# Pair products split into a rounded half and a remainder, with layer 0 in three fp32r products

## The chip, the cores and the metric

The kernel runs on 1 core of one Trainium2 chip. The metric is the device time in microseconds, the median of several executions; lower is better. The profiler followed one further execution of the kernel before.

## The reference

A batch of 1024 rows has 39 fields, each an embedding of 16 numbers that is looked up in its own table. A compressed interaction network of three layers combines them, and a small network follows.

```
x0 = e                       # (1024, 39, 16), gathered from 39 tables
for W in (f0, f1, f2):       # f0 (39*39, 128), f1 and f2 (128*39, 128)
    z  = einsum('bfd,bgd->bfgd', x0, xk).reshape(b, f*g, d)
    xk = einsum('bpd,pm->bmd', z, W)
    outs.append(xk)
z = sum(concatenate(outs, 1), -1)          # (1024, 384)
h = relu(concatenate([z, dense_ctx], 1) @ W_top1 + b_top1)
h = relu(h @ W_top2 + b_top2)
y = h @ W_top3
```

## The kernel before, in words

The batch is cut into 8 batch tiles of 128 rows (index bt), each batch tile into 4 groups of 32 rows (index q; g = 4*bt + q counts the 32 groups), and each group into 4 tiles of 8 rows (index j; t counts the 128 tiles). Eight rows times 16 embedding numbers fill the 128 partitions of a tile. Every engine runs a list of instructions written out by hand, and semaphores tie the lists together.

**Layer 0** uses the symmetry of x times x. The 39*40/2 products of two fields are laid out in 7 blocks (k = 0 to 6) of up to 117 partitions: `pairs[k] = x shifted by k fields * base`, 512 columns wide (32 rows times 16). SyncE copies `base` and the six `shifted` blocks of each group by DMA. GpSimd multiplies them (`pair`, L347); for the first group VectorE does it (L536). TensorE sums the seven blocks into bank C, one fp32 matmul each, with the folded filter `f0_sum` (`cur0_sum`, L655); the trace has two records for each such matmul. The matmuls for group g + 1 are put into group g's list at the slots AT_SUM = 12, 15, ..., 30 of 40 slots. `pairs` is a ring of 3, and a product waits for the sum that frees its place.

**The split of cur0.** ScalarE rounds the sum to fp32r (`cur0_high`, L423), and VectorE takes the remainder (`cur0_low`, L540) and the sum over the 16 embedding numbers for the output (`z0`, L542). ScalarE does it in tile 3 at c = 1, VectorE there ahead of the reduction of unit 2.

**Layer 1** is the bulk. Per tile there are 10 chunks (c = 0 to 9) of 4 fields, a slot each: TensorE multiplies cur0 with f1 in three fp32r matmuls of 512 columns (L707, L708, L709) into one of 6 PSUM banks. Two chunks form a unit. The chunks of units 0, 2 and 4 are scaled by x on ScalarE (L436), and VectorE reduces the unit (L577, L585, L596). The other chunks are scaled and added by VectorE itself (`fuse`, L572, alternating between `sum_a` and `sum_b`). L587 adds the reduced unit 2 to `sum_a`, and L593 adds `sum_a` and `sum_b` into the last unit. TensorE may write a unit again once VectorE has read what stood there three units earlier; chunk 4 of a tile waits for L596 of the tile before.

**Layer 2 and the rest.** For each tile, `g_product` (L663) multiplies the result with `x_block`, which GpSimd spreads from `x_col` (L331, four instructions for a group); ScalarE copies it to G (L428, at c = 5). Layer 2 (L669) sums over 39 fields, 13 in each of the groups q = 1, 2, 3 of the next batch tile, in bank C; the small network uses bank C in the groups with q = 0, and once more in the last group. The first instruction of a group waits for `cur0_low`, and a use of bank C also for `z0`.

**Loading.** GpSimd gathers the rows of the next batch tiles (L320, 39 indirect DMAs for a batch tile), spread over the tiles. SyncE repeats the gathered rows by DMA (L291), and TensorE transposes them in the group with q = 2 (L629; L714 for the first batch tile, copied from PSUM at L399 and L522). At the start SyncE issues 50 loads of f0 and ScalarE 47 more of its mirror (L227), and the weights f2, w1 and w2 follow on SyncE ahead of the first copies of x.

Of the kernel before, what the change touches and what calls it, by code (L numbers as in the profile page):

```python
# [5 lines left out]
F32 = mybir.dt.float32  # L6
F32R = mybir.dt.float32r
# [26 lines left out]
RING = 3  # L34
# [19 lines left out]
AT_SUM = [12 + 3 * k for k in range(K0)]  # L54
# [6 lines left out]
EARLY = 16  # L61
AHEAD = 10
# [52 lines left out]
def gathers_in_tile(t):  # L115


    step, u = divmod(t + AHEAD, TPB)
    if step == 0:
        n, tiles = NF - EARLY, TPB - AHEAD  # L120
        return 1, range(EARLY + n * t // tiles, EARLY + n * (t + 1) // tiles)
    if step + 1 >= BT:
        return None
    return step + 1, range(NF * u // TPB, NF * (u + 1) // TPB)


def build(nc, dense, ids, tables, w1, b1, w2, b2, w3, f0, f1, f2, out):
    ctx = ExitStack()
    with ctx:
# [12 lines left out]
        f0_sum = sb("f0_sum", [SEL, K0, M])  # L142
# [11 lines left out]
        rows = sb("rows", [P, 2, SEQ * D])  # L154
# [4 lines left out]
        pairs = sb("pairs", [SEL, RING, GN])  # L159
        cur0_high = sb("cur0_high", [P, 2, GN], F32R)  # L160
# [5 lines left out]
        part = sb("part", [P, 2, M])  # L166
# [6 lines left out]
        dense_sb = G[:, FC * P + K0 * M:FC * P + K0 * M + BT * D].rearrange("p (t c) -> p t c", t=BT)  # L173
# [5 lines left out]
        y = sb("y", [1, B])  # L179
# [6 lines left out]
        gathered = [sem("gathered_even"), sem("gathered_odd")]  # L186
        consts_made, block_ready, ones_set = sem("consts_made"), sem("block_ready"), sem("ones_set")
        mirror_zero, f0_in, f0_ready = sem("mirror_zero"), sem("f0_in"), sem("f0_ready")
        f1_in, f1_high_ready, f1_ready = [sem(f"f1_in{i}") for i in range(3)], sem("f1_high_ready"), sem("f1_ready")
# [3 lines left out]
        first_repeat, repeated, x_read = sem("first_repeat"), sem("repeated"), sem("x_read")  # L193
        based = [sem("based_even"), sem("based_odd")]
        copied = [sem(f"copied{k}") for k in range(1, K0)]
        first_pairs, pairs_ready = sem("first_pairs"), sem("pairs_ready")
        cur0_summed, cur0_high_ready, cur0_ready = sem("cur0_summed"), sem("cur0_high_ready"), sem("cur0_ready")
# [25 lines left out]
        def load_f0(eng, mirrored):  # L223
            for mirror, k, p0, n, first, step in pieces:
                if mirror == mirrored:
                    dst = (f0_mirror if mirror else f0_sum)[p0:p0 + n, k, :]
# [15 lines left out]

        def base_copy(eng, g, j):
# [3 lines left out]

        def shift_copy(eng, g, k):
            cols = x_cols(*divmod(g, QG))
            r = K0_ROWS[k]  # L250
            eng.dma_start(shifted[0:r, k - 1, :], cols[k:k + r, :]).then_inc(copied[k - 1], 16)
# [4 lines left out]
        def _(sp):  # L256
            sp.dma_start(ids_sb[:], ids.rearrange("(t p) f -> p t f", p=P)).then_inc(ids_in, 16)
            load_f0(sp, False)
            sp.dma_start(f2_sb[:], f2.rearrange("(f g) m -> g f m", g=M)).then_inc(f2_in, 16)
# [562 lines left out]
```

## Time and profile before

| | |
|---|---|
| median of 3 runs | 1467.61 us (1467.0 to 1467.76) |
| the profiled execution, its own time | 1464.04 us |
| its span | 1462.3 us |
| mean granted TensorE clock | 0.971 |
| busy: PE, DVE, ACT, POOL | 92%, 83%, 62%, 46% |

PE is TensorE, PEld its weight loads, DVE VectorE, ACT ScalarE, POOL GpSimd and SP SyncE. Times are in microseconds from the start of the span. L587 is line 587 of the kernel before. Matmuls are pipelined and their ends are modelled, so distances between starts say more than durations.

### The profile page before, as it was taken

What the parts mean: (1) busy time and instruction counts of PE and PEld (TensorE: products, weight loads), DVE (VectorE), ACT (ScalarE), POOL (GpSimd) and SP (SyncE); (2) the same over time, 40 slices, a digit from 0 to 9 for tenths busy, and PEclk for the clock granted to TensorE, in tenths of its full rate; (3) what the DMA queues carried; (4) which work ended last, traced back from release to release, by engine and by line L of the source; (5) the groups of instructions that cost most, each with busy time, mean ns of one, the idle gap of its engine ahead of it and who ended that gap; (6) DMA issues with size and microseconds to landing.
All of it is one profiled execution on the core that took longest, in us unless ns stands there. A gap on an engine that the chain in (4) does not pass through costs nothing.

```text
span 1462.3 us, 20057 instructions
## 1 busy us (share of the span) xinstructions
PE 1344.7 (92%) x5856; PEld 1001.8 (69%) x5856; DVE 1212.5 (83%) x2792; ACT 907.2 (62%) x3233; POOL 676.1 (46%) x666
## 2 busy tenths in 40 slices
PE   0059999999999999999999999999999998988998
PEld 0036676667777777777777777777777676766677
DVE  0249999998989999899889989898989989898874
ACT  0226776666666676667666676666766665655563
POOL 6737656554445555554545547354545423123200
PEclk8579999999999999999999999999999999999999
DMA  7131212120300212010210202101210202010000
GB/s 181 35 109 29 66 45 69 27 65 3 92 27 21 66 50 63 27 52 16 80 33 27 65 21 85 34 26 42 73 40 27 64 1 94 21 38 24 1 1 1
DMA packets 54456, 67.28 MB, mean 46 GB/s; under 512 B 13927, under 2 KB 25945, under 8 KB 54346
## 3 DMA queue, kind: packets, MB, share of 16 engines
q1 hardware_dynamic: 36811, 59.70, 12.9%
q0 software_dynamic: 9984, 2.58, 1.6%
q10 hardware_dynamic: 7551, 3.72, 1.0%
q8 instruction: 47, 0.77, 0.2%
q14 instruction: 63, 0.52, 0.1%
HBM read 10.02 MB, written 0.00 MB: 7 GB/s over the span
## 4 chain that ended last, share of the span: by engine, by line
PE 69%; DVE 17%; issue 5%; ACT 5%; ACTq 2%; another core or an unknown queue 1%; DMA 0%; SPq 0%; DVEq 0%
PE Y L707 16%; PE Y L709 14%; PE Y L708 14%; PE C L655 9%; PE C L669 5%; PE S L663 5%; DVE sum_b L572 4%; ACT Y L436 4%; DVE cur L596 4%; DVE sum_a L572 3%; DVE Y L593 2%; DVE part L585 2%; ACTq L227 2%; PE S L629 1%
## 5 line engine op out<-in xcount | busy, mean ns | idle before, releaser
L436 ACT ACTIVATE Y<-Y,x_col 128x128 f32<-128x128 f32 x2944 | 800.8, 356 | 447.2 <-PE Y L709 415.9
L707 PE MATMUL Y<-f_high,cur_high 128*128 128x512 f32 (+1 forms) x1280 | 627.6, 490 | 32.2 <-DVE cur L596 23.2
L709 PE MATMUL Y<-f_high,cur_low 128*128 128x512 f32 (+1 forms) x1280 | 500.1, 391 | 0.0
L708 PE MATMUL Y<-f_low,cur_high 128*128 128x512 f32 (+1 forms) x1280 | 499.6, 390 | 0.0
L347 POOL TENSOR_TENSOR pairs<-shifted,base 117x512 f32<-117x512 f32 x186 | 241.0, 1296 | 548.5 <-PE C L655 546.6
L572 DVE SCALAR_TENSOR_TENSOR sum_a<-Y,x_col,sum_a 128x128 f32<-128x128 f32 x1024 | 349.6, 341 | 13.9 <-issue 0.5
L707 PEld LDWEIGHTS Y<-f_high,cur_high 128*128 128x128 f32 x1280 | 242.4, 189 | 171.0 <-DVE cur L596 57.9
L320 POOL DMA_INDIRECT rows<-in_tbl_dram,ids_sb x312 | 304.1, 975 | 72.4 <-issue 58.9
L572 DVE SCALAR_TENSOR_TENSOR sum_b<-Y,x_col,sum_b 128x128 f32<-128x128 f32 x896 | 305.1, 341 | 0.5 <-DVE sum_a L572 0.4
L708 PEld LDWEIGHTS Y<-f_low,cur_high 128*128 128x128 f32 x1280 | 243.1, 190 | 84.9 <-issue 47.4
L709 PEld LDWEIGHTS Y<-f_high,cur_low 128*128 128x128 f32 x1280 | 241.5, 189 | 51.7
L655 PE MATMUL C<-pairs,f_sum 117*128 117x512 f32 (+1 forms) x448 | 230.0, 596 | 6.7 <-DVE pairs L536 6.7
L585 DVE TENSOR_REDUCE part<-Y 128x128 f32<-128x1024 f32 x128 | 156.5, 1223 | 74.3 <-ACT Y L436 72.1
L577 DVE TENSOR_REDUCE sum_a<-Y 128x128 f32<-128x1024 f32 x128 | 155.9, 1218 | 35.2 <-ACT Y L436 34.7
L596 DVE TENSOR_REDUCE cur<-Y 128x128 f32<-128x1024 f32 x128 | 156.7, 1224 | 4.4
L655 PEld LDWEIGHTS C<-pairs,f_sum 117*128 117x128 f32 (+1 forms) x448 | 84.7, 192 | 29.7 <-issue 10.2
L331 POOL TENSOR_TENSOR x_block<-x_col,block 128x320 f32<-128x320 f32 x128 | 91.3, 745 | 9.0 <-ACT x_col L417 8.5
L587 DVE TENSOR_TENSOR sum_a<-sum_a,part 128x128 f32<-128x128 f32 x128 | 88.7, 693 | 4.4
L663 PE MATMUL S<-x_block,cur 128*128 128x320 f32 x256 | 92.2, 442 | 0.0
L669 PEld LDWEIGHTS C<-G,f_sb 128*128 128x128 f32 x624 | 84.0, 196 | 10.1 <-issue 3.6
L669 PE MATMUL C<-G,f_sb 128*128 128x128 f32 x624 | 86.1, 280 | 1.4 <-ACT G L428 0.6
L593 DVE TENSOR_TENSOR Y<-sum_a,sum_b 128x128 f32<-128x128 f32 x128 | 66.9, 523 | 14.0 <-ACT Y L436 0.8
(73 smaller groups left out, 554.6 us busy)
## 6 DMA issues: line engine op xcount, KB each, us to landing
shifted<-x_seq SPq DMA_DIRECT2D x157, 234.0 KB
base<-x_seq SPq DMA_DIRECT2D x96, 78.0 KB
rows<-in_tbl_dram,ids_sb POOLq DMA_INDIRECT x312
shifted<-x_seq SPq DMA_DIRECT2D x32, 156.0 KB
rows<-rows SPq DMA_DIRECT2D x14, 312.0 KB
G<-in_L_rec_f_dram ACTq DMA_DIRECT2D x3, 832.0 KB
w_sb<-in_W_top_dram SPq DMA_DIRECT2D x1, 768.0 KB
shifted<-x_seq ACTq DMA_DIRECT2D x3, 234.0 KB
```

Of the source, the lines that this page charges most:

```text
L320: pool.indirect_dma_start(out=rows[:, bt % 2, f * D:(f + 1) * D], out_offset=None, in_=tables[f], in_offset=bass.IndirectOffsetOnAxis(ap=i ...
L347: pool.tensor_tensor(pairs[0:r, z % RING, :], shift, base[0:r, g % 2, :], ALU.mult)\
L436: ins = act.activation(where[:, i * M:(i + 1) * M], where[:, i * M:(i + 1) * M], ACT.Copy, scale=x_col[:, t // JT % QG, t % JT, f:f + 1])
L572: dve.scalar_tensor_tensor(acc, src, x, acc, ALU.mult, ALU.add).then_inc(acc_steps, 1)
L585: dve.tensor_reduce(part[:, t % 2, :], unit(t, 2), AX.X, ALU.add).then_inc(acc_steps, 1)
L596: dve.tensor_reduce(cur1[:, t % 2, :], unit(t, 4), AX.X, ALU.add).then_inc(acc_steps, 1)
L655: pe.matmul(C[:], f0_sum[0:r, k, :], pairs[0:r, z % RING, :], start=k == 0, stop=k == K0 - 1).then_inc(cur0_summed, 1)
L663: pe.matmul(S[:, 0:TB * FC], cur1[:, t % 2, :], x_block[:, t // JT % 2, t % JT, :], start=True, stop=True).then_inc(s_filled, 1)
L669: ins = pe.matmul(C[:, 0:P], f2_sb[:, f, :], half[:, f, :], start=f == first, stop=f == end - 1)
L707: pe.matmul(where, ch, wh, start=True, stop=False)
L708: pe.matmul(where, ch, wl, start=False, stop=False)
L709: pe.matmul(where, cl, wh, start=False, stop=True).then_inc(y_filled, 1)
```

## The change

Each pair product is now kept in three forms: the product in fp32 (`pairs`), its rounded half in fp32r (`pairs_high`, made by ScalarE) and the remainder (`pairs_low`, subtracted by GpSimd, for the first group by VectorE). The folded filter is split in the same way (`f0_sum` and `f0_low`). A layer-0 sum is three fp32r matmuls instead of one fp32 matmul. All three rings have 2 places. The sums stand at slots 12, 15, 19, 23, 27, 31, 35, ScalarE rounds at AT_ROUND, and cur0's split moves from c = 1 to c = 5 of tile 3 on ScalarE and behind `fuse(t, 6)` on VectorE.

```diff
-RING = 3
+RING = 2
-AT_SUM = [12 + 3 * k for k in range(K0)]
+AT_SUM = [12, 15, 19, 23, 27, 31, 35]
+AT_ROUND = {(0, 1): 0, (0, 5): 1, (1, 1): 2, (1, 5): 3, (2, 1): 4, (2, 5): 5, (3, 1): 6}
+            def pair_low(g, k):
+                z = K0 * g + k
+                r = K0_ROWS[k]
+                pool.wait_ge(pairs_rounded, z + 1)
+                pool.tensor_tensor(pairs_low[0:r, z % RING, :], pairs[0:r, z % RING, :],
+                                   pairs_high[0:r, z % RING, :].bitcast(F32), ALU.subtract).then_inc(low_ready, 1)
+            LOW_STEPS = ((("pair", 0), ("pair", 1), ("low", 0), ("pair", 2), ("low", 1)),
+                         (("pair", 3), ("low", 2), ("pair", 4), ("low", 3)),
+                         (("pair", 5), ("low", 4), ("pair", 6), ("low", 5)),
+                         (("low", 6),))
...
+            def round_pair(g, k):
+                z = K0 * g + k
+                r = K0_ROWS[k]
+                if g:
+                    act.wait_ge(pairs_ready, z - K0 + 1)
+                else:
+                    act.wait_ge(first_pairs, k + 1)
+                if z >= RING:
+                    act.wait_ge(cur0_summed, z - RING + 1)
+                act.activation(pairs_high[0:r, z % RING, :], pairs[0:r, z % RING, :], ACT.Copy)\
+                   .then_inc(pairs_rounded, 1)
...
                         if c == 1:
                             if q == 2 and bt + 1 < BT:
                                 read_transposes(bt + 1, j)
-                            if j == JT - 1 and g + 1 < NG:
-                                split_cur0(g + 1)
                             if with_mlp:
                                 relu1(mlp, mlp + 1)
                         if c == AT_G:
+                            if j == JT - 1 and g + 1 < NG:
+                                split_cur0(g + 1)
                             if t:
                                 read_g(t - 1)
                             if with_mlp:
                                 relu2(mlp, mlp + 1)
+                        if (j, c) in AT_ROUND and g + 1 < NG:
+                            round_pair(g + 1, AT_ROUND[j, c])
...
                 fuse(t, 3, FUSE3, 0)
                 if j == 0 and q and g >= QG:
                     layer2_read(g // QG - 1, q - 1)
-                if j == JT - 1 and g + 1 < NG:
-                    split_cur0(g + 1)
                 dve.wait_ge(scaled, NSC * t + 4)
-                dve.tensor_reduce(part[:, t % 2, :], unit(t, 2), AX.X, ALU.add).then_inc(acc_steps, 1)
+                dve.tensor_reduce(part[:], unit(t, 2), AX.X, ALU.add).then_inc(acc_steps, 1)
                 dve.wait_ge(acc_steps, n0 + R1)
-                dve.tensor_tensor(sum_a[:, t % 2, :], sum_a[:, t % 2, :], part[:, t % 2, :], ALU.add)\
+                dve.tensor_tensor(sum_a[:, t % 2, :], sum_a[:, t % 2, :], part[:], ALU.add)\
                    .then_inc(acc_steps, 1)
                 fuse(t, 6, FUSE6, 1)
+                if j == JT - 1 and g + 1 < NG:
+                    split_cur0(g + 1)
                 fuse(t, 7, FUSE7, 1)
...
-                pe.matmul(C[:], f0_sum[0:r, k, :], pairs[0:r, z % RING, :],
-                          start=k == 0, stop=k == K0 - 1).then_inc(cur0_summed, 1)
+                high, low = pairs_high[0:r, z % RING, :], pairs_low[0:r, z % RING, :]
+                pe.matmul(C[:], f0_sum[0:r, k, :], high, start=k == 0, stop=False)
+                pe.matmul(C[:], f0_low[0:r, k, :], high, start=False, stop=False)
+                pe.matmul(C[:], f0_sum[0:r, k, :], low, start=False, stop=k == K0 - 1).then_inc(cur0_summed, 1)
```

These parts of the change stand in words:

- GpSimd goes through LOW_STEPS with a gather between two steps. A pair product waits for the remainder that used its place before, a rounding for the sum that did. Gathers of a batch tile keep out of tiles 2 and 3 of the group with q = 1.
- The gathered rows are kept once (`rows`). Four GpSimd copies (`take_rows`, in those tiles 2 and 3) put them into `rows_seq` in the order of the embedding numbers; SyncE's three repeating DMAs for a batch tile are gone. For the first batch tile ScalarE, VectorE (two) and GpSimd make the four copies.
- At the start, GpSimd issues 4 gathers of batch tile 1 behind its copy, waits for the first copies of x, issues two shift copies itself, and only then the 12 gathers that remain. ScalarE takes one base copy and two shift copies, SyncE two and two.
- ScalarE rounds f1 first and issues the 47 loads of f0's mirror behind that. VectorE adds f0 and copies the first rows ahead of f1's remainder. For the first group VectorE takes turns: pair product k, then remainder k - 1.
- The loads of f2, w1 and w2 move on SyncE from ahead of the first copies to behind group 1's shift copies.
- `y` holds one batch tile, and ScalarE sends it out for each, where SyncE sent it twice at the end.

## Rows read from the trace of the kernel before

**Rows 1.** The page: busy time and share of each engine, and the chain by engine.
```profile
PE 1344.7 (92%) x5856; PEld 1001.8 (69%) x5856; DVE 1212.5 (83%) x2792; ACT 907.2 (62%) x3233; POOL 676.1 (46%) x666
...
PE 69%; DVE 17%; issue 5%; ACT 5%; ACTq 2%; another core or an unknown queue 1%; DMA 0%; SPq 0%; DVEq 0%
```

**Rows 2.** Windows, one batch tile each: length, then PE, PEld, DVE, ACT, POOL busy.
```profile
918.20:1085.10 166.90, 165.54 (x733) 123.76 (x732) 148.31 (x348) 112.46 (x403) 85.43 (x83) 1.00 0.15 45
1085.10:1260.00 174.90, 167.67 (x734) 124.76 (x732) 156.16 (x349) 112.45 (x403) 59.80 (x57) 0.99 0.14 42
```

**Rows 3.** Timeline, tile 1 of group 15: start, us, engine, line, operation.
```profile
724.62 1.12 ACT L436 ACTIVATE Y<-Y,x_col 128x128 f32<-128x128 f32 x4 [1.43 <-PE Y L709]
...
727.73 0.46 ACT L428 ACTIVATE G<-S 128x320 f32<-128x320 f32 x1
...
727.87 1.23 DVE L585 TENSOR_REDUCE part<-Y 128x128 f32<-128x1024 f32 x1 [0.90 <-ACT Y L436]
...
727.92 1.02 PE L655 MATMUL C<-pairs,f_sum 117*128 117x512 f32 x2
...
729.01 0.40 PE L708 MATMUL Y<-f_low,cur_high 128*128 128x512 f32 x1
...
729.24 0.40 PE L709 MATMUL Y<-f_high,cur_low 128*128 128x512 f32 x1
```

**Rows 4.** Waits between 120 and 1390 us: total, times, longest.
```profile
ACT Y L436 <- PE Y L709: 391.9, 333, 6.6
...
PEld Y L707 <- DVE cur L596: 55.4, 56, 4.7
```

**Rows 5.** By line, L587 and L540: duration in ns, min/median/max.
```profile
L587 DVE TENSOR_TENSOR sum_a<-sum_a,part x128: 291/293/2095, 106.2 to 1438.5; 128x128 f32<-128x128 f32 x128
...
L540 DVE TENSOR_TENSOR cur_low<-C,cur_high x32: 678/680/692, 96.6 to 1394.6; 128x512 fp32r<-128x512 f32 x32
```

**Rows 6.** Timeline, groups 15 and 27: DVE's additions and POOL's products.
```profile
729.03 1.30 POOL L347 TENSOR_TENSOR pairs<-shifted,base 117x512 f32<-117x512 f32 x1 [0.53 <-PE C L655]
...
729.13 1.34 DVE L587 TENSOR_TENSOR sum_a<-sum_a,part 128x128 f32<-128x128 f32 x1
...
1235.92 4.55 DVE L593 TENSOR_TENSOR Y<-sum_a,sum_b 128x128 f32<-128x128 f32 x1
...
1236.33 2.76 POOL L331 TENSOR_TENSOR x_block<-x_col,block 128x320 f32<-128x320 f32 x4
...
1239.06 1.25 POOL L347 TENSOR_TENSOR pairs<-x_seq,base 117x512 f32<-117x512 f32 x1
```

**Rows 7.** Groups by form from 584.4 to 751.2 us: busy, mean ns.
```profile
L587 DVE TENSOR_TENSOR sum_a<-sum_a,part 128x128 f32<-128x128 f32 x16 | 12.0, 748 | 0.5
...
L593 DVE TENSOR_TENSOR Y<-sum_a,sum_b 128x128 f32<-128x128 f32 x16 | 5.8, 362 | 1.7
```

**Rows 8.** Timeline, DVE in tile 3 of group 14.
```profile
707.39 0.68 DVE L540 TENSOR_TENSOR cur_low<-C,cur_high 128x512 fp32r<-128x512 f32 x1
707.99 0.68 DVE L542 TENSOR_REDUCE z<-C 128x32 f32<-128x512 f32 x1
```

**Rows 9.** Timeline, the start up to the first chunk.
```profile
1.33 21.03 SPq L227 DMA_DIRECT2D f_sum<-in_L_rec_f_dram  x50
...
9.64 40.73 ACTq L227 DMA_DIRECT2D G<-in_L_rec_f_dram  x47
...
57.11 0.70 ACT L396 ACTIVATE rows<-rows 128x624 f32<-128x624 f32 x1
...
60.46 3.65 PE L714 MATMUL Y<-ident,rows 128*123 128x128 f32 x16 [37.42 <-DVE rows L518]
...
75.29 0.95 POOL L320 DMA_INDIRECT rows<-in_tbl_dram,ids_sb  x1 [0.31 <-issue]
...
79.81 0.29 DVE L522 COPY x_seq<-Y 123x128 f32<-123x128 f32 x1 [16.96 <-remote]
...
97.48 0.54 PE L707 MATMUL Y<-f_high,cur_high 128*128 128x512 f32 x1 [1.70 <-DVE cur_low L540]
```

More of the change, by code:

```diff
@@ L61 @@
 EARLY = 16
+FIRST_EARLY = 4
 AHEAD = 10
@@ L344, in pair @@
                 else:
-                    pool.wait_ge(copied[k - 1], 16 * (g + 1))
+                    pool.wait_ge(copied[k - 1], 16 * (g if k in POOL_COPIES else g + 1))
                     shift = shifted[0:r, k - 1, :]
+                if g == 1 and k < RING:
+                    pool.wait_ge(first_low, K0)
+                else:
+                    pool.wait_ge(low_ready, z - K0 - RING + 1)
                 pool.tensor_tensor(pairs[0:r, z % RING, :], shift, base[0:r, g % 2, :], ALU.mult)\
                     .then_inc(pairs_ready, 1)
+            def pair_low(g, k):
[8 more added lines that the diff above has]
+                         (("low", 6),))
             pool.wait_ge(ids_in, 16)
             gather(0, range(NF))
-            gather(1, range(EARLY))
+            pool.wait_ge(gathered, 16 * NF)
+            pool.tensor_copy(*row_part(2 * NF, NF)).then_inc(first_rows, 1)
+            pool.wait_ge(first_rows, 4)
+            gather(1, range(FIRST_EARLY))
+            pool.wait_ge(first_read, 4)
+            for k in POOL_COPIES:
+                shift_copy(pool, 0, k)
+            gather(1, range(FIRST_EARLY, EARLY))
             pool.wait_ge(ones_set, 1)
@@ L361, in _ @@
                     fs = list(now[1]) if now else []
-                    if now and now[0] == 2 and now[1][0] == 0:
-                        pool.wait_ge(first_filled, 4)
-                    elif now and now[0] > 2 and now[1][0] == 0:
-                        pool.wait_ge(s_filled, S_USE["x", now[0] - 2, JT - 1] + 1)
-                    ks = ((0, 1, 2), (3, 4), (5, 6), ())[j] if g + 1 < NG else ()
-                    for i in range(max(len(ks), len(fs))):
-                        if i < len(ks):
-                            pair(g + 1, ks[i])
+                    if now and now[0] > 1 and now[1][0] == 0:
+                        pool.wait_ge(rows_taken, len(ROW_PARTS) * (now[0] - 1))
+                    if q == 1 and j >= 2 and bt + 1 < BT:
+                        for part in ((0, 1), (2, 3))[j - 2]:
+                            take_rows(bt + 1, part)
+                    steps = LOW_STEPS[j] if g + 1 < NG else ()
+                    for i in range(max(len(steps), len(fs))):
+                        if i < len(steps):
+                            kind, k = steps[i]
+                            (pair if kind == "pair" else pair_low)(g + 1, k)
                         if i < len(fs):
@@ L402, in _ @@
             act.wait_ge(first_read, 4)
-            for k in (1, 3, 5):
+            base_copy(act, 0, 2)
+            for k in (1, 3):
                 shift_copy(act, 0, k)
```

177 lines of the change are left out of this document (110 added, 67 removed).

## The prediction

> **What bounds the kernel now.** I read the shares and the chain first. PE is busy for 92% of the span and holds 69% of the chain, DVE 83% and 17% [rows 1]. Then the stretches by batch tile of 16 tiles: the four from 417.5 to 1085.1 us take 166.8 to 167.0 us each, with PE at 165.4 to 165.5 and DVE at 148.0 to 149.2; the last of them is shown [rows 2]. PE's ends are modelled, so I counted its work by the distance from start to start. An fp32r product of 512 columns follows the last after 0.23 us, three make a chunk of 0.70 us, and an fp32 pair sum stands 0.86 us ahead of the next chunk's first product (from 727.92 us to 729.01 less the 0.23 that lie between 729.01 and 729.24) [rows 3]. A batch tile has 160 chunks (16 x 6.9 = 110), 16 G products of 0.53 (8.5), 28 pair sums (24), 39 layer-2 products of about 0.23 (9), the transposes of x and of the scalars (5.5) and the small network (6): about 162.5. So PE is idle for only 4.4 us of 167, and it spends them behind DVE: the longest of PE's waits, 55.4 us in 56 waits of its weight loads, is for the final reduce of L596 [rows 4]. The second engine is close behind the first, and what either waits for counts.
>
> The last view is how long DVE's two additions take whose operands all lie in SBUF. L587 has a minimum of 291 and a maximum of 2095 ns, while L540, which reads PSUM and SBUF, stays at 678 to 692 [rows 5]. The timeline shows why: L587 starts 0.10 us after a pair product of POOL and ends just behind it, 1.34 us long, and an L593 lasts 4.55 us through the rest of one pair product, four x_block products and the next pair product, which follow without a gap [rows 6]. In an undisturbed batch tile L587 and L593 have means of 748 and 362 ns [rows 7] against some 293 and 300 when nothing blocks them, so DVE loses 16 x (0.455 + 0.062) = 8.3 us. The price is in rows 2: from 918.2 to 1085.1 DVE is busy for 148.3 of 166.9 us, from 1085.1 to 1260.0 for 156.2 of 174.9. That is 7.9 us more for DVE and 8.0 more for the kernel: a blocked microsecond is paid about one to one.
>
> **Part 1, the pair sums on PE.** Three fp32r products at 0.23 replace one fp32 product: 0.86 - 0.70 = 0.16 us, 28 times in a batch tile: -4.4 us. The bounds are 0 (if the third weight load showed) and 0.16, which is what the chunks next to it show, so I take 0.16. The Trainium skill (FP8 and Floating Point Precision, on fp32 precision) says that true FP32 takes four passes through the array. By that rule a sum would fall from 0.86 to 0.64 and save 6 us in a batch tile; the chunks here show 0.70 for three.
>
> **Part 2, the later split of cur0.** Sum 6 moves from slot 30 to slot 35 of 40, and cur0's split from before the reduce L585 to behind fuse(6). Before, the split was over when PE came to the boundary: cur_low at 707.39, z at 707.99 [rows 8], a good microsecond ahead of the next group's first product. Now the chain starts at the end of chunk 35: ACT scales it (1.2, from the four in 1.12 us of rows 3), DVE reduces unit 2 (1.24), adds (0.3), fuses four (4 x 0.26), takes cur_low (0.68) and z (0.68): 4.5 us to cur_low, 5.2 to z. PE has 3 x 0.70 + 0.58 + 0.3 = 3.0 us of its own there. It idles 1.5 us where only cur_low is needed, and 2.2 where layer 2 or the small network needs bank C, which z must have read; from the second batch tile on that is every group. Against it I set 0.5 us of the idle that PE has now in such a tile and that falls away once DVE catches up at the boundary: +1.7 us for each of four groups, +6.8. Parts 1 and 2 make +2.4 for a batch tile. What is queued behind PE's wait is all of the next group.
>
> **Part 3, the remainder on POOL.** 28 subtractions of 117x512 in a batch tile. POOL's product of that shape takes 1.30 us [rows 6]; a subtraction isn't in the trace, and DVE's addition in L587 (128x128) against such a product can't tell more, so 1.30 with bounds 1.2 and 1.5. POOL goes from 85.4 us of 166.9 [rows 2] to about 122, and 127 with the copies of rows: not the bound. But where they lie matters. In tiles 0 to 2, ACT rounds a pair right behind G in slot c = 5, and POOL's subtraction starts as that ends. From G's start: G 0.46, the rounding 0.68 (as cur_low, which has its width [rows 8]; it is on ACT, so some hundredths may go either way), and POOL follows after 0.1: subtraction at +1.2. DVE's reduce L585 starts 0.14 after G, at 727.87 against 727.73, and L587 comes at 729.13, that is +1.4 us [rows 3, 6]. So L587 finds POOL at work for another 1.1 us, three times in four tiles and locked in phase, since both chains start from the same scaled chunk: 12 x 1.05 = 12.6 us. In tile 3 x_block's four products (2.8 us) and pair 0 now come when DVE wants L587, and a hit there delays cur_low: I put 4 us for a batch tile, and 1 for L593. Together 17.6 against the present 8.3: +9.3. I take two thirds, +6.2, since PE has a few tenths in hand in tiles 0 and 2; bounds 0 (POOL starts after L587) and 25 (each hit lasts 2.1, as the longest L587, and x_block is hit in each group).
>
> **Part 4, costed at nothing.** 28 roundings of 0.6 on ACT are 17 us on 112.5 of 167 [rows 2]; the cover is the 391.9 us in which ACT waits for PE's chunks [rows 4]. If POOL is late, ACT holds back the scaling behind the rounding, and DVE and PE after it (a rival below). The 21 row DMAs of SP become 28 POOL copies in tiles without gathers. y's eight DMAs move to ACT, 0.4 us each by SP's 50 loads in 21.03 us [rows 9], in that same idle time. The loads of f2, w1 and w2 move behind group 1's shift copies on SP; nothing is queued behind them until group 2's copies a whole group later, and f2 is first read in group 5.
>
> **Part 5, the start.** Now the first chunk comes at 97.48. PE's transposes of L714 end at 64.1, yet the last copy that waits for them starts at 79.81, with a releaser that the trace doesn't know. POOL issues gathers 1.25 us apart all through, the last at 75.29 [rows 9]. The trace doesn't say what holds the copies. In the changed kernel only 4 gathers stand there, so either the stall shrinks to some 4 us (gain 12.5) or it stays. The rows are ready at 58.7 instead of 60.4, where L714 starts: ACT's copy shows at 57.11 that the last gather has landed [rows 9], then comes POOL's copy, some 1.6 us by 1.30/512 an element (-1.7). The chain from the first copies to the first chunk, 17.7 us now, grows: seven pairs and seven remainders of some 0.69 on DVE (9.7 us) against about 7.3 us that the trace now has for seven pairs and their sums, and half a microsecond more for the last sum: +3. ACT's 47 mirror loads take 40.7 us from 9.64 [rows 9]; they now start at about 15, and end at 56, just in time for the rows. Their bounds are 35 (all at the pace of SP, 50 in 21.03 us [rows 9]) and 75 (47 at 1.28, about what a gather's issue holds POOL). So -11 or +1, evenly: -5.
>
> **The sum.** A batch tile +2.4 + 6.2 = +8.6. Seven of the eight count (the first has no layer 2, the last no pair products at its end): +60. The start -5: +55. The profiled execution took 1464.0 us with a span of 1462.3; the median of three is 1467.6, 3.6 longer. 1464 + 55 + 3.6 = 1522 us.
>
> **Rivals.** *PE is all that counts* (faster, 0.23): the boundary's wait is made up because DVE's present waits fall into it. Then 31 x 7 x 0.16 = 35 us are gained, with the start 46: down to 1422, and about 1445 if half is lost. For it: PE is at 99% between 417 and 1085 us. Against: DVE's chain behind chunk 35 is longer than PE's work. It decides if the boundary idles under 1 us and blocked DVE time stays under 8.3 us for a batch tile. *The boundary alone* (0.19): the remainders miss L587. 7 x 2.4 = +17, less 5: 1480, from 1464 to 1496. *POOL holds up more* (0.18): it comes late to the remainder, so that ACT stands before the scaling, or x_block's four products and pair 0 (4.1 us) stand before cur_low in three groups of four. 3 us x 3 x 7 = +63 on the forecast: 1585. For it: rows 6 show such a block. Against: the gathers between POOL's products, which split such runs. My forecast has 0.40 (1500 to 1550).
>
> **Numbers.** A difference under 0.2% can't be told from none here. Slower 0.72 (forecast, last rival and most of the second), within it 0.05, faster 0.23. The range takes in the second rival and the dearer half of the first, and most of the last: 1450 to 1585.
>
> **What would show it.** Right: three products 0.23 apart for each pair sum; PE idle 1.5 to 2.2 us at each group's start, released by cur_low or z; a mean of L587 above 1.1 us, its long ones behind the subtractions; stretches of 172 to 178 us for a batch tile. Wrong: a stretch under 167, a mean of L587 under 0.75, or the long waits on ACT's roundings instead. For the start, whether the copies behind the first transposes follow at once.

## The result and the profile after

The changed kernel takes 1575.28 us (median of four runs, 1566.91 to 1578.25), the kernel before 1467.3 on the same chip: a ratio of 1.0731, 95% interval 1.071 to 1.0752. The change makes the kernel 108 us slower; 55 were forecast, in a range from 1450 to 1585.

The page of the changed kernel, which answers to [rows 1]: spans, busy time and share of each engine, the granted clock in 40 slices, and the chain by engine.

```profile
PE 1374.9 (87%) x6080; PEld 1059.7 (67%) x6080; DVE 1235.3 (78%) x2801; ACT 1024.9 (65%) x3459; POOL 987.5 (63%) x914
...
PEclk8589999999989999999999999899989999899999
...
PE 44%; DVE 34%; issue 13%; ACT 7%; SPq 1%; POOL 1%; DMA 0%; DVEq 0%; ACTq 0%; POOLq 0%
```

PE's share of the chain falls from 69 to 44% and DVE's doubles, though DVE's own work hardly grew: the two now stand in turn on one path. POOL takes all of the 311 us that were put on it and still has over a third of the span free.

Windows of the changed kernel, batch tiles 4 and 6, as in [rows 2] (length, then PE, PEld, DVE, ACT, POOL, granted clock):

```profile
808.80:992.90 184.10, 169.69 (x760) 130.98 (x760) 151.08 (x347) 126.75 (x431) 125.41 (x115) 0.96 0.13 37
...
1176.40:1367.80 191.40, 174.83 (x760) 136.01 (x760) 152.66 (x347) 126.72 (x431) 101.72 (x92) 0.93 0.12 36
```

A batch tile takes 184.1 us where it took 166.9, and PE stands idle for 14 of them. PE's busy time rose although its work fell: the clock is at 0.96 instead of 1.00, so some products run at the lower level. Within a group of four tiles most of the time is lost in one place. From start to start, tiles 0 to 3 of a group took 10.5, 10.4, 10.9 and 9.9 us in the kernel before; in the changed one they take 11.3, 10.7, 9.6 and 14.3 (means of the 16 groups of batch tiles 2 to 5, from the traces).

The waits of the changed kernel between 120 and 1500 us (total, times, longest), as in [rows 4]:

```profile
POOL pairs_low L379 <- ACT pairs_high L476: 421.3, 174, 16.9
ACT Y L494 <- PE Y L800: 395.7, 268, 7.6
DVE sum_a L669 <- ACT Y L494: 110.0, 32, 10.4
...
PEld C L760 <- DVE cur_low L632: 50.8, 20, 3.2
PE C L760 <- DVE z L634: 45.0, 20, 3.0
```

The last three rows are the group's boundary seen from both engines: PE waits 2 to 3 us for the split of cur0 in L632 and L634, and then DVE waits 3.4 us in each of 32 places for the first scaled chunk of the new group. POOL waiting for ACT's roundings is idle time of an engine that bounds nothing.

The boundary itself, tile 3 of group 14 in the changed kernel's timeline, to set beside [rows 8]:

```profile
755.88 1.11 ACT L494 ACTIVATE Y<-Y,x_col 128x128 f32<-128x128 f32 x4 [0.95 <-PE Y L800]
...
757.02 1.22 DVE L675 TENSOR_REDUCE part<-Y 128x128 f32<-128x1024 f32 x1 [0.86 <-ACT Y L494]
...
758.28 0.41 DVE L677 TENSOR_TENSOR sum_a<-sum_a,part 128x128 f32<-128x128 f32 x1
...
758.61 0.34 PE L800 MATMUL Y<-f_high,cur_low 128*128 128x384 f32 x1
...
759.65 0.67 DVE L632 TENSOR_TENSOR cur_low<-C,cur_high 128x512 fp32r<-128x512 f32 x1
...
760.25 0.67 DVE L634 TENSOR_REDUCE z<-C 128x32 f32<-128x512 f32 x1
...
761.07 1.13 PE L760 MATMUL C<-G,f_sb 128*128 128x128 f32 x8 [2.13 <-DVE z L634]
```

PE's last product ends at 758.95, layer 2's first starts at 761.07: 2.13 us idle, released by z. One group later the small network stands there. The same timeline, the window that holds the granted clock, and for comparison the ten microseconds behind the wait shown first:

```profile
804.27 0.76 PE L768 MATMUL C<-z_dense,w_dense 16*128 16x128 f32 x2 [2.08 <-DVE z L634]
...
808.56 0.77 PE L798 MATMUL Y<-f_high,cur_high 128*128 128x512 f32 x1
...
809.13 0.63 PE L799 MATMUL Y<-f_low,cur_high 128*128 128x512 f32 x1
...
809.56 0.63 PE L800 MATMUL Y<-f_high,cur_low 128*128 128x512 f32 x1
...
810.23 1.11 ACT L494 ACTIVATE Y<-Y,x_col 128x128 f32<-128x128 f32 x4 [6.91 <-PE Y L800]
```

```profile
801.00:811.00 10.00, 7.92 (x30) 5.86 (x30) 5.65 (x14) 2.95 (x13) 7.30 (x8) 0.66 0.10 26
...
761.00:771.00 10.00, 9.93 (x56) 8.58 (x57) 6.95 (x17) 5.87 (x19) 6.68 (x6) 1.00 0.39 119
```

Around the 2.08 us without a product the clock goes down: products of 512 columns stand 0.43 us apart, not 0.23 as in [rows 3]. That is 1.2 GHz in place of 2.4. All the while ACT has no chunk to scale (6.91 us) and DVE none to fuse. Behind the wait of 2.13 us at 761.07 the clock stayed at 1.00. Of the changed kernel's 31 boundaries, 19 have half clock at the wait or just behind it, and 12 don't; in batch tiles 2 to 5 the waits of both kinds last 2.0 to 2.1 us, so their length alone doesn't decide.

### The profile page after: what moved, and what is told of

It is laid out like the page before. It is cut to its first block, busy times and chain, and to the rows that moved or that the text cites. A ratio compares the mean times of both kernels' runs of the same rounds, so it can differ in the third digit from the quotient of the medians.

```text
span 1575.1 us, 21208 instructions
## 1 busy us (share of the span) xinstructions
PE 1374.9 (87%) x6080; PEld 1059.7 (67%) x6080; DVE 1235.3 (78%) x2801; ACT 1024.9 (65%) x3459; POOL 987.5 (63%) x914
## 3 DMA queue, kind: packets, MB, share of 16 engines
q1 hardware_dynamic: 33640, 54.64, 11.3%
## 4 chain that ended last, share of the span: by engine, by line
PE 44%; DVE 34%; issue 13%; ACT 7%; SPq 1%; POOL 1%; DMA 0%; DVEq 0%; ACTq 0%; POOLq 0%
PE Y L798 10%; DVE sum_b L664 8%; PE Y L800 8%; PE Y L799 8%; DVE part L675 7%; DVE cur L688 7%; ACT Y L494 6%; DVE sum_a L664 6%; PE C L760 6%; PE S L754 4%; DVE Y L685 2%; DVE cur_low L632 1%; DVE z L634 1%; PE C L745 1%; PE C L769 1%
## 5 line engine op out<-in xcount | busy, mean ns | idle before, releaser
L798 PE MATMUL Y<-f_high,cur_high 128*128 128x512 f32 (+1 forms) x1280 | 556.7, 435 | 64.1 <-DVE cur L688 47.8
L379 POOL TENSOR_TENSOR pairs_low<-pairs,pairs_high 117x512 fp32r<-117x512 f32 (+1 forms) x217 | 279.2, 1287 | 422.4 <-ACT pairs_high L476 421.8
L799 PE MATMUL Y<-f_low,cur_high 128*128 128x512 f32 (+1 forms) x1280 | 505.8, 395 | 0.0
L800 PE MATMUL Y<-f_high,cur_low 128*128 128x512 f32 (+1 forms) x1280 | 505.7, 395 | 0.0
L799 PEld LDWEIGHTS Y<-f_low,cur_high 128*128 128x128 f32 x1280 | 247.3, 193 | 40.6
L476 ACT ACTIVATE pairs_high<-pairs 117x512 fp32r<-117x512 f32 (+1 forms) x224 | 151.0, 674 | 10.6 <-PE C L747 4.7
L760 PE MATMUL C<-G,f_sb 128*128 128x128 f32 x624 | 99.6, 309 | 48.1 <-DVE z L634 47.5
L760 PEld LDWEIGHTS C<-G,f_sb 128*128 128x128 f32 x624 | 96.3, 222 | 62.2 <-DVE cur_low L632 53.6
L677 DVE TENSOR_TENSOR sum_a<-sum_a,part 128x128 f32<-128x128 f32 x128 | 126.2, 986 | 4.4
L745 PE MATMUL C<-pairs_high,f_sum 117*128 117x512 f32 (+1 forms) x224 | 103.9, 464 | 10.6 <-DVE pairs_low L608 8.6
```

The costliest lines, as they stand in the source:

```text
L379: pool.tensor_tensor(pairs_low[0:r, z % RING, :], pairs[0:r, z % RING, :], pairs_high[0:r, z % RING, :].bitcast(F32), ALU.subtract).then_i ...
L760: ins = pe.matmul(C[:, 0:P], f2_sb[:, f, :], half[:, f, :], start=f == first, stop=f == end - 1)
L798: pe.matmul(where, ch, wh, start=True, stop=False)
L799: pe.matmul(where, ch, wl, start=False, stop=False)
L800: pe.matmul(where, cl, wh, start=False, stop=True).then_inc(y_filled, 1)
```

## The experiments

The start differs from chip to chip, not only from kernel to kernel. The kernel before takes 1447 to 1449 us on two chips and 1467 where it was first timed and where e9 to e12 ran; some 16 of the 19 us lie ahead of its first chunk (97.5 or 81 us). So runs are compared by their ratio to the kernel before on the same chip, and, best, by the middle of the kernel: the mean stretch of batch tiles 2 to 5, from the first product of chunk 0 to that of the next batch tile. It is 166.9 us before and 183.3 after. "Us at half clock" counts from 100 us on, in the profiled execution.

**e5: the changed kernel on a chip of the faster kind.**

> The changed kernel itself, beside the kernel before on the same chip as the next three. In the run of the boundary alone the start is the one of the kernel before, and its first chunk came at 81 us, not 97.5: the 16 us behind the first transposes weren't there. Theory (that stall belongs to an execution or a chip, not to the program): the changed kernel starts its first chunk at 81 to 89 us while the kernel before does so at 81, so it gains nothing at the start, and where the kernel before takes 1448 us the ratio is 1.08 to 1.09. Rival (the changed kernel sheds a stall of its own in such a run too): a ratio of 1.073 again.

Measured: 1571.24 us, ratio 1.0856 (1.0828 to 1.0883), stretch 184.0. The first chunk starts at 84.3 us, against 81.1 with the start of the kernel before (e4). The theory held: of the 16 us nothing is left to gain there.

**e4: the boundary alone, on the kernel before.** The slots of the change for the sums, and ACT's rounding and DVE's split in the places that the change gives them; of DVE:

```diff
-AT_SUM = [12 + 3 * k for k in range(K0)]
+AT_SUM = [12, 15, 19, 23, 27, 31, 35]
...
-                if j == JT - 1 and g + 1 < NG:
-                    split_cur0(g + 1)
                 dve.wait_ge(scaled, NSC * t + 4)
...
                 fuse(t, 6, FUSE6, 1)
+                if j == JT - 1 and g + 1 < NG:
+                    split_cur0(g + 1)
```

> The kernel before with the second part of the change alone: pair sums in slots 12, 15, 19, 23, 27, 31, 35 instead of 12 to 30, ACT's rounding of cur0 at chunk 5 of tile 3 and DVE's split behind fuse(6); the sums stay one fp32 product each and there is no remainder. The prediction put this part at 6.8 us for a batch tile, 48 us in all, 1515 us. Theory now (DVE comes later to the boundary than assumed and the clock halves behind PE's idle time): 70 to 120 us more than before, 1540 to 1585, with well over 100 us at half clock. Rival (the boundary is cheap, POOL's remainders make the loss): 1475 to 1490 us.

Measured: 1526.38 us, ratio 1.0533 (1.0515 to 1.0551), 78 us more; stretch 180.9, that is +14.0; 107 us at half clock against 23 before. The 78 us lie in the theory's 70 to 120, at their low end; the rival fell. Its windows row, one batch tile:

```profile
780.80:961.30 180.50, 170.97 (x731) 128.86 (x731) 144.19 (x347) 112.45 (x403) 85.49 (x83) 0.96 0.14 42
```

With POOL's work as in the kernel before (85.5 us), PE idles for 9.5 us and runs at 0.96. Set beside [rows 2], PE idles 8.2 us more and is busy 5.4 us longer over the same products. No remainder is needed to lose most of what the change loses. One thing went the other way: the two additions of DVE are held up less here. In the same window, by form (busy, mean ns):

```profile
L593 DVE TENSOR_TENSOR Y<-sum_a,sum_b 128x128 f32<-128x128 f32 x16 | 7.0, 437 | 1.7
...
L585 DVE TENSOR_TENSOR sum_a<-sum_a,part 128x128 f32<-128x128 f32 x16 | 5.6, 352 | 0.5
```

L585 of this kernel is L587 of the kernel before, which had 748 [rows 7]: some 3 us a batch tile are blocked, not 8.3. The experiment moves sums and split together and doesn't tell which of them does that.

**e1: the split moved ahead, in the changed kernel.**

```diff
                 dve.tensor_reduce(part[:], unit(t, 2), AX.X, ALU.add).then_inc(acc_steps, 1)
+                if j == JT - 1 and g + 1 < NG:
+                    split_cur0(g + 1)
                 dve.wait_ge(acc_steps, n0 + R1)
                 dve.tensor_tensor(sum_a[:, t % 2, :], sum_a[:, t % 2, :], part[:], ALU.add)\
                    .then_inc(acc_steps, 1)
                 fuse(t, 6, FUSE6, 1)
-                if j == JT - 1 and g + 1 < NG:
-                    split_cur0(g + 1)
```

> The changed kernel with one thing moved on DVE: in the last tile of a group cur0's split (cur_low and z) stands right behind the reduce of unit 2, ahead of the addition of L677 and the four steps of fuse(6). Theory (the boundary is dear: PE stands idle for cur_low and z, and then runs the next chunks at the half clock): cur_low comes 1.3 us earlier in each of 31 groups, 40 us by itself and up to 65 with the clock, so 1510 to 1535 us, tile 3 of a group 1.3 to 2 us shorter, and less than 183 us at half clock. Rival (what counts is DVE's whole work together with the blocked additions, and the order within it doesn't): less than 10 us.

Measured: 1481.15 us, ratio 1.0223 (1.0206 to 1.024): 90 us less than the changed kernel's 1571 on such a chip, more than the theory's highest figure; the rival fell. Stretch 172.9, and only 9 us at half clock. Its boundary in the timeline, and a batch tile's window:

```profile
722.71 0.68 DVE L632 TENSOR_TENSOR cur_low<-C,cur_high 128x512 fp32r<-128x512 f32 x1
...
723.15 0.34 PE L800 MATMUL Y<-f_high,cur_low 128*128 128x384 f32 x1
...
724.14 1.13 PE L760 MATMUL C<-G,f_sb 128*128 128x128 f32 x8 [0.65 <-DVE z L634]
```

```profile
768.30:940.80 172.50, 163.65 (x761) 126.07 (x760) 152.73 (x348) 126.69 (x431) 125.51 (x116) 1.00 0.14 40
```

PE idles 0.65 instead of 2.13 us and its clock stays up (no boundary of this run has half clock); PE's busy time falls by 6.0 us with the same products. DVE is just as busy as in the changed kernel, so its total work wasn't what counted.

**e9: idle time filled with products that bring nothing.** Changed kernel, PE, at each group's start:

```diff
+                        if g:
+                            v = UNITS * t - UB
+                            pe.wait_ge(cur0_high_ready, g + 1)
+                            pe.wait_ge(acc_steps, NST * (v // UNITS) + FREED[2 * (v % UNITS)])
+                            for _ in range(6):
+                                pe.matmul(bank(t, 0)[:, 0:4 * M], cur0_high[:, g % 2, 0:P],
+                                          f1_high[:, 0:4, :].rearrange("p f m -> p (f m)"), start=True, stop=True)
                         pe.wait_ge(cur0_ready, g + 1)
```

> The changed kernel with six needless products of 512 columns on PE between cur_high and the wait for cur_low at each group's start; chunk 0 overwrites what they write, so they bring nothing forward. Theory (part of the boundary's price is the granted clock, which falls to half behind PE's idle time): the clock rises from 0.95 to 0.97 or more and 10 to 40 us are saved, by work that does nothing else. Rival (the clock follows something else, or its half rate costs nothing since DVE sets the pace): no gain, or up to 15 us more where the six products last beyond cur_low.

Measured: 1531.6 us, ratio 1.0445 (1.0422 to 1.0469) on a chip where the kernel before takes 1467.04, so some 43 us less than the changed kernel; stretch 177.9. The window of a batch tile, to set beside the changed kernel's above:

```profile
791.30:969.20 177.90, 169.14 (x785) 130.36 (x783) 150.99 (x348) 127.10 (x431) 125.67 (x116) 1.00 0.14 39
```

PE runs 24 products more in it, which bring nothing forward, and is busy for 0.6 us less, at a clock of 1.00. These 43 us, 1.4 for each of 31 boundaries, are the price of the clock by itself, as far as these products keep it up (18 us at half clock are left, of 128). It lay just above the expectation.

**e8: the idle time put to use.** Changed kernel; two products each of chunks 0 and 1 need cur_high only. DVE's read of layer 2 moves behind the reduce of unit 2. Of PE:

```diff
+            def early_products(t, g):
+                for c in (0, 1):
...
+                    pe.matmul(where, ch, f1_high[:, lo:hi, :].rearrange("p f m -> p (f m)"), start=True, stop=False)
+                    pe.matmul(where, ch, f1_low[:, lo:hi, :].rearrange("p f m -> p (f m)"), start=False, stop=False)
...
                     if s == 0:
+                        if g:
+                            pe.wait_ge(cur0_high_ready, g + 1)
+                            early_products(t, g)
                         pe.wait_ge(cur0_ready, g + 1)
...
-                    if q and bt and s < len(L2_SLICES):
+                    if q and bt and 2 <= s < 2 + len(L2_SLICES):
```

> The changed kernel with PE's idle time at a group's start put to use: the first two products of chunks 0 and 1, which need only cur_high, stand ahead of the wait for cur_low, and layer 2's slices begin at chunk 2, so that its wait for z comes later, with DVE's read of them behind the reduce of unit 2. DVE's split stays where it is. Theory (PE's idle time at the boundary is what costs, in itself and by the clock): 0.9 us in each of 31 groups and half of the time at half clock, 40 to 75 us less. Rival (DVE's chain sets the pace, and its next tile can't begin before cur_low anyway): 15 us less at most, though with a higher clock.

Measured: 1504.95 us, ratio 1.0401 (1.0368 to 1.0435), 66 us less; stretch 174.9, 52 us at half clock. Useful products give back most of the clock (128 us at half before the edit) and save some 20 us more than e9. The rival fell.

**e2: a short remainder.** Changed kernel, POOL, 16 of 512 columns:

```diff
-                pool.tensor_tensor(pairs_low[0:r, z % RING, :], pairs[0:r, z % RING, :],
-                                   pairs_high[0:r, z % RING, :].bitcast(F32), ALU.subtract).then_inc(low_ready, 1)
+                pool.tensor_tensor(pairs_low[0:r, z % RING, 0:16], pairs[0:r, z % RING, 0:16],
+                                   pairs_high[0:r, z % RING, 0:16].bitcast(F32), ALU.subtract).then_inc(low_ready, 1)
```

> The changed kernel with POOL's remainder taken of 16 of the 512 columns of a pair; the other columns of the remainder keep old values, which leaves that part of the computation out. Everything waits for the same things in the same order. Theory (POOL's 1.3 us remainders block the addition of L677 in tiles 0 to 2): the mean of L677 falls from 0.99 to below 0.5 us and the time by 45 to 75 us. Rival (only the boundary counts, where L677 is hit least, 0.47 us in tile 3): 15 us at most, with L677 as short.

**e3: additions with an operand in PSUM.** Changed kernel, all of POOL's work as it is. The two additions now follow each other at the tile's end, and chunk 7's bank comes free with the second:

```diff
                     acc = (sum_a, sum_b)[(i + starts) % 2][:, t % 2, :]
+                    if c > 3 and i % 2:
+                        acc = part[:]
...
-                        dve.scalar_tensor_tensor(acc, src, x, acc, ALU.mult, ALU.add).then_inc(acc_steps, 1)
+                        to = src if c == 7 and i > 1 else acc
+                        dve.scalar_tensor_tensor(to, src, x, acc, ALU.mult, ALU.add).then_inc(acc_steps, 1)
...
-                dve.wait_ge(acc_steps, n0 + R1)
-                dve.tensor_tensor(sum_a[:, t % 2, :], sum_a[:, t % 2, :], part[:], ALU.add)\
-                   .then_inc(acc_steps, 1)
...
-                dve.tensor_tensor(bank(t, 9)[:, SUM_SLOT * M:], sum_a[:, t % 2, :], sum_b[:, t % 2, :], ALU.add)\
+                dve.tensor_tensor(sum_a[:, t % 2, :], bank(t, 7)[:, 3 * M:4 * M], sum_a[:, t % 2, :], ALU.add)\
+                   .then_inc(acc_steps, 1)
+                dve.wait_ge(acc_steps, n0 + JOIN)
+                dve.tensor_tensor(bank(t, 9)[:, SUM_SLOT * M:], bank(t, 7)[:, 2 * M:3 * M], sum_a[:, t % 2, :],
+                                  ALU.add)\
```

> The changed kernel with the work of POOL as it is, and DVE's two additions given one operand in PSUM each: from chunk 6 on, the partial sum of the reduce is used as third accumulator instead of sum_a, the last step on it and on sum_b is written back to PSUM in place, and the two additions follow each other at the tile's end. Theory (only additions with both operands in SBUF are blocked by POOL): no addition over 0.5 us, 85 of the 95 blocked microseconds gone, and the time 30 to 60 us less, since part of it goes back to PE's bound. Rival (whatever DVE writes to SBUF is held up by POOL): the additions stay long, 0.6 us or more in the mean, and the time within 10 us.

Measured: e2 1494.42 us, ratio 1.0299 (1.0246 to 1.0353), 77 us less, stretch 177.8; e3 1492.22 us, ratio 1.0282 (1.0249 to 1.0316), 79 us less, stretch 175.7. e3 falls further than its 60, e2 just below its 75, with a mean of L677 of 0.44 us; both rivals fell. e2 keeps the boundary's wait and 114 us at half clock, e3 has 63. Now the additions, by line (duration in ns, min/median/max). First the changed kernel, as in [rows 5], then e2, then e3:

```profile
L677 DVE TENSOR_TENSOR sum_a<-sum_a,part x128: 291/1101/2876, 98.4 to 1551.6; 128x128 f32<-128x128 f32 x128
```

```profile
L677 DVE TENSOR_TENSOR sum_a<-sum_a,part x128: 291/293/1394, 91.0 to 1473.2; 128x128 f32<-128x128 f32 x128
```

```profile
L685 DVE TENSOR_TENSOR sum_a<-Y,sum_a x128: 290/292/294, 93.8 to 1468.6; 128x128 f32<-128x128 f32 x128
...
L688 DVE TENSOR_TENSOR Y<-Y,sum_a x128: 299/299/300, 94.1 to 1468.9; 128x128 f32<-128x128 f32 x128
```

The median of the addition rose from 293 to 1101 ns with the remainders and is back at 293 without them, which settles that they do it. e3 shows what kind of instruction is hit: with POOL as busy as ever, 256 additions that read one operand from PSUM don't vary by more than 4 ns. It isn't that they moved out of POOL's way: 94 of them overlap one of its two-input instructions, and none is longer for it, while of the changed kernel's 128 L677 118 overlap one and 110 are longer than 350 ns. The Trainium skill (SBUF — State Buffer, Who interferes with whom) says so: a DVE instruction with two inputs in SBUF contends with POOL's reads, one with at most one such input doesn't; the trace agrees. How the hit looks, in the changed kernel's timeline:

```profile
747.31 1.73 DVE L677 TENSOR_TENSOR sum_a<-sum_a,part 128x128 f32<-128x128 f32 x1
...
747.59 1.29 POOL L379 TENSOR_TENSOR pairs_low<-pairs,pairs_high 117x512 fp32r<-117x512 f32 x1
```

**e6: three products for each sum, on the kernel before.** Pairs and filter are held as fp32r. The second and third product have a filter of zeros, so both remainders are left out, and POOL and ACT do nothing more:

```diff
-                pe.matmul(C[:], f0_sum[0:r, k, :], pairs[0:r, z % RING, :],
-                          start=k == 0, stop=k == K0 - 1).then_inc(cur0_summed, 1)
+                pe.matmul(C[:], f0_sum[0:r, k, :], pairs[0:r, z % RING, :], start=k == 0, stop=False)
+                pe.matmul(C[:], f0_zero[0:r, :], pairs[0:r, z % RING, :], start=False, stop=False)
+                pe.matmul(C[:], f0_zero[0:r, :], pairs[0:r, z % RING, :],
+                          start=False, stop=k == K0 - 1).then_inc(cur0_summed, 1)
```

> The kernel before with the first part of the change alone on PE: pairs and filter are taken as fp32r and every pair sum is three products of 512 columns, of which the second and third have a zero filter (the remainders of pairs and filter are left out of the computation, POOL and ACT do nothing for them), in the slots of before. Theory (PE bounds the kernel before, 0.16 us a sum): 217 sums by 0.16, 35 us less at most, 15 us less at least as DVE is close behind. Rival (DVE and its blocked additions set the pace by now): within 5 us of before.

Measured: 1422.28 us, ratio 0.9827 (0.9805 to 0.9848), 25 us less, inside the theory's 15 to 35; stretch 164.3, -2.6. A sum and the chunk behind it in the timeline:

```profile
738.88 0.40 PE L658 MATMUL C<-pairs,f_sum 117*128 117x512 f32 x1
...
739.35 0.40 PE L660 MATMUL C<-pairs,f_zero 117*128 117x512 f32 x1
739.58 0.40 PE L712 MATMUL Y<-f_high,cur_high 128*128 128x512 f32 x1
```

**e7: the additions beside PSUM, on the kernel before.** The edit is e3's.

> The kernel before with DVE's two additions given an operand in PSUM, as was done to the changed kernel: 80 us of blocked additions in the kernel before should go. Theory (a blocked microsecond of DVE costs most of one): 15 to 40 us less, down to PE's own work. Rival (PE is at 99% in the undisturbed stretches, so only the 8 us of the disturbed one come back): 10 us less at most.

Measured: 1410.96 us, ratio 0.9751 (0.9735 to 0.9767), 36 us less. Every stretch from the third on takes 164.9 us, the last one too, which took 174.9 [rows 2]. The undisturbed ones give back only 2.0 of 8.3 blocked microseconds, the disturbed one 10 of its 16, and the last batch tile, which has as many, with the end behind it 16. So the time is the theory's 15 to 40 us less, but nearly three quarters of it come from two batch tiles; for the undisturbed stretches the rival was nearer.

**e10 and e11: the repairs together.** e10 is the changed kernel with e1 and e3, e11 with e8's products besides.

> The changed kernel with cur0's split moved ahead of the addition and fuse(6), and with DVE's additions beside PSUM: the two repairs together. By themselves they saved 90 and 79 us against the changed kernel's 1571. Theory (they share the boundary: the early split goes around the blocked addition anyway, so the second repair gives only the 8 to 10 us a batch tile of tiles 0 to 2): 1400 to 1430 us. Rival (what is left is PE waiting for remainders of POOL before sums 5 and 6, which neither mends): above 1440 us.

> The two repairs together and the first two products of chunks 0 and 1 ahead of the wait for cur_low, with layer 2 from chunk 2 on. Theory (some 2 us of idle PE stay at each boundary with the early split, of which 0.9 us are filled): 15 to 28 us less than with the two repairs alone, 1375 to 1415 us, which would beat the kernel before with its additions beside PSUM (1411). Rival (DVE's chain from cur_low on sets the pace): within 5 us of the two repairs alone.

Measured beside a kernel before of 1467.04 us: e10 1447.59 us, ratio 0.9874 (0.9854 to 0.9895), stretch 168.2; e11 1430.28 us, ratio 0.9759 (0.974 to 0.9778), stretch 165.5. The first product of e10's chunk 0 stands at 90.0 us there, 5 to 7 us later than in e1 and e3 on another chip (84.8 and 82.9), e11's at 88.2; without these e10 comes to about 1441 and lies above its expected 1430, just where the rival begins, and e11 to about 1426, over its 1415. The 17 us between them are as expected. In e10's batch tile 4 PE is busy for 161.4 of 167.8 us, and its weight loads wait 6.8 us for remainders, in 8 waits; 3.1 us of it are idle time of PE too:

```profile
PEld C L749 <- POOL pairs_low L379: 6.8, 8, 1.0
...
PE C L749 <- POOL pairs_low L379: 3.1, 7, 0.5
```

That is the rival's mechanism, and with four boundaries of 0.65 us it makes up most of the 6.4 us for which PE idles there. So both halves of the expectation for e10 are partly right. With e11 the repaired change stands level with e7 (stretches of 165.5 and 164.9 us), which is an edit of a few lines on the kernel before, and the fastest kernel of this study.

**e12: e7 with the early products.** Their edit is e8's.

> The kernel before with its additions beside PSUM (1411 us) and the first two products of chunks 0 and 1 ahead of the wait for cur_low, with layer 2 from chunk 2 on. There cur_low is over a microsecond early. Theory (a boundary without idle time has nothing to fill): within 5 us of 1411. Rival (PE does lose some 0.5 us at each boundary there, behind z): 10 to 15 us less.

Measured: 1460.31 us, ratio 0.9959 (0.9944 to 0.9973); stretch 169.2, 4.3 more than e7. Both theories missed. The waits from 560 to 720 us:

```profile
PEld Y L708 <- issue: 5.3, 4, 1.5
...
PE Y L708 <- DVE part L586: 4.1, 4, 1.2
```

The early products wait a microsecond in each of four groups for the reduce of unit 2 in the tile before, which frees their bank. In e7 layer 2's slice stood in that place and needed no bank.

## Why the prediction was right or wrong

The direction was right, the size was half of what was measured, and the time lies in the range because the range was stretched to 1585 for a rival whose mechanism didn't come: that part is luck. Of the signs that were named, the products 0.23 us apart and PE's idle time of 1.5 to 2.2 us released by cur_low or z are there; the stretch went over its 172 to 178 and the mean of L677 stayed under its 1.1 us. Per batch tile, in the middle of the kernel:

| part | forecast | measured | by |
|---|---|---|---|
| 1, sums | -4.4 | -2.6 | e6 |
| 2, boundary | +6.8 | +14.0 | e4 |
| 3, remainders | +6.2 | +5.0 | what is left of 183.3 - 166.9 |
| sum | +8.6 | +16.4 | |

- **Part 1** had the right price: a sum's three products take 0.70 us to the next chunk's first (0.86 before). Only 2.6 of 4.4 us arrive; that PE then waits more for DVE is likely and not shown. The Trainium skill (FP8 and Floating Point Precision, TensorE Precision Notes) gives true FP32 four passes through the array; the estimate worked out from that in the prediction was 0.64 us for a sum, and e6's rows have 0.70. The terms by which the prediction counts PE's work add up to 163 us and not 162.5; nothing hangs on it.
- **Part 2 is the step that failed**, and not in its chain. It said 4.5 us from chunk 35 to cur_low and 5.2 to z; the timeline has 4.48 (755.84 to 760.32) and 5.08. It said 2.2 us of idle PE behind z, and 2.13 is there. What it put at nothing, without a reason, is what such an idle time does next: at 19 of 31 boundaries the clock halves, and chunk 0, on which ACT and DVE wait, comes late twice over. Per group it forecast 1.7, and e4 has 14.0 / 4 = 3.5. e4's window splits that: 8.2 / 4 = 2.0 are more idle time, 5.4 / 4 = 1.4 the same products at a lower clock, and e9 gives the same 1.4 for the clock in the changed kernel. So the clock is the larger miss, and of the 0.5 us that was set against the wait little came.
- **Part 3** said L677 would be blocked for 1.05 us in tiles 0 to 2, locked in phase. Its mean rose to 923 ns in batch tile 3, against 748 [rows 7]; in tiles 0, 1 and 2 of the middle groups it is 0.94, 1.11 and 1.34 us, so their blocking is 10 us a batch tile, near the 12.6 forecast. In tile 3 it is 0.36: of the 4 us put there 0.3 came. And L685 is freed of most of its hits (mean 328), so the blocked time is 10.5 us and not 17.6. A blocked microsecond doesn't cost one everywhere: 2.0 of 8.3 come back in the kernel before (e7), 7.6 of 10.5 in the changed one (e3, which also takes the addition out of the chain to cur_low). The 5.0 in the table is a remainder of e4, where only 3 us are blocked: 7.5 more blocked microseconds cost 5.0, which is two thirds of them. The forecast took its two thirds of a growth of 9.3 above the 8.3 of the kernel before, where 2.2 came. Two sizes were off and nearly cancelled.
- **Part 4** at nothing held. ACT's roundings fit: POOL waits for them, and no long wait of PE or DVE names them.
- **Part 5** said -11 or +1 and took -5. With its stall the kernel before started at 97.48, the changed one at 88.67 (-8.8); without it (e4, e5) 81.1 and 84.3 (+3.2). So both cases are real, each on its chips, and each some 2 us later than forecast; the -5 was the mean of two cases of which neither is near it. The first copies of the changed kernel follow at once:

```profile
65.92 0.29 DVE L588 COPY x_seq<-Y 123x128 f32<-123x128 f32 x1 [2.16 <-PE Y L805]
67.24 0.29 DVE L588 COPY x_seq<-Y 123x128 f32<-123x128 f32 x1 [1.03 <-PE Y L805]
```

- **Over the whole run**, from trace to trace: the first seven batch tiles take 117 us more where 60 were forecast, the last one with the end 5 more, and the start 9 less. The middle doesn't show all. Added to 1447, e6 and e4 make 1500, and the changed kernel takes 1571 (e5). By its stretches some 23 of the other 71 lie in the four middle ones, 3 in the start, and some 18 in the first two batch tiles, 13 in the seventh and 12 in the last with the end, which weren't taken apart; the seventh alone takes 191.4 (174.9 before).
- **The rivals.** *POOL holds up more* gave 1585, near the time, by the wrong mechanism: ACT waits for PE, not before its roundings, and with every block of DVE gone (e3) a stretch still takes 175.7. *The boundary alone* named the dearest part and priced it at 2.4 net instead of 11.4. *PE is all that counts* named its own test, a boundary that idles under 1 us, and 2.1 us are there.

The repairs overlap only in part. Against the changed kernel e1 saves 90 us, e3 79, e8 66 and e9 43; by their stretches e1 saves 10.4, e3 7.6, and both together (e10) 15.1 of 16.4. The boundary's wait comes from the order of DVE's list and not from blocked additions: in the middle PE idles 2.1 us there in the changed kernel, still 1.7 with no addition blocked (e3, where the addition is out of that chain), and 0.65 with the split moved ahead (e1, e10). The blocked time lies in tiles 0 to 2.

## What to carry to other kernels

When an edit puts a chain behind the work of the engine that bounds the kernel, price not only the microseconds that it idles but what follows: a clock at half rate and every engine behind it, here 1.4 us on top of 2.0 in each group. Before moving work from PE to others, look at the instruction that PE's next stage waits for, and put that first in its queue (90 us for moving two instructions, e1). And give each DVE addition one operand in PSUM where POOL is busy: 2.5% for the kernel before.

## What the runs showed of the hardware

- TensorE's clock was at half around 19 of 31 idle times of the changed kernel, most of them some 2 us long (2.08 in the rows above), and stayed up around 12, among them the one of 2.13. It was also at half around 11 of e3's, all of 1.7 us, and around none of e1's and e10's, of 0.65 us in the middle. Six needless products in that place kept it up: 0.96 to 1.00 in the mean, and 43 us (e9).
- A DVE addition of 128x128 with both inputs in SBUF took up to 2876 ns beside POOL's products, with one in PSUM 290 to 300, in 512 cases (e3, e7), of which 213 overlap a two-input instruction of POOL.
- The stall at the start went with the chip. The kernel before had its second copy at 79.81 us, and e12, with the same start, at 79.63 on a chip where the kernel before is as slow, with a releaser unknown to the trace, while on another chip (e4) the same copy ran at once when the transposes were done, under the same gathers 1.25 us apart:

```profile
62.34 0.29 DVE L522 COPY x_seq<-Y 123x128 f32<-123x128 f32 x1 [1.28 <-PE Y L714]
```

What it is stays open.
